# Layer 1 of a two-layer mixture of experts: gate columns of all tiles first, sixteen x buffers, fourteen tiles through the row ring

## The reference

```
x = x + 0.5 * ffn(layernorm(x))        # "layer 0"
x = x + attn(layernorm(x))             # linear recurrence over time ("mamba")
x = x + 0.5 * ffn(layernorm(x))        # "layer 1", the same weights

ffn(x):
  scores = sigmoid(gate_w @ x) + gate_b              # 16 experts
  weights, indices = top_k(scores, 4); weights /= sum
  shared = silu(x @ w1s) * (x @ w3s) @ w2s           # hidden 176
  h_e = silu((x @ w1_e) * (x @ w3_e))                # 16 experts, hidden 176
  out = shared + sum over the 4 chosen e of weight_e * (h_e @ w2_e)
```

## Time and profile before

| | |
|---|---|
| runs | 560.19, 560.35, 562.23 us, median 560.35 |
| profiled execution | 561.91 us, its span 560.1 us, mean granted TensorE clock 0.922 |
| busy share of the span | PE 86%, DVE 78%, ACT 66%, POOL 63% |
| DMA | 88.27 MB, 158 GB/s over the span |
| chain that ended last | PE 60%, DVE 16%, issue 10%, DMA 5%, POOL 4%, ACT 4% |
| layer 1 | front from 306, routing to 360.4, routed loop to 529, end to 560.1 us |

### The profile page before, as it was taken

One profiled execution on the slowest core, in us unless ns is written; L12 is line 12 of the kernel. 1 busy time (PEld: TensorE's weight loads), 2 busy tenths in 40 slices (PEclk: granted clock), 3 DMA queues, 4 the chain that ended last, 5 costly groups with the idle time before them and its releaser, 6 DMA issues.

```text
span 560.1 us, 13322 instructions
## 1 busy us (share of the span) xinstructions
PE 481.5 (86%) x3206; PEld 449.0 (80%) x3207; DVE 436.5 (78%) x1464; ACT 367.2 (66%) x1109; POOL 352.7 (63%) x364
## 2 busy tenths in 40 slices
PE   2969569999999999958996960599999999999865
PEld 2857449999999999947884950389999999999754
DVE  5889857777889888875998579656777888887836
ACT  2687836777777777767874571656777777777610
POOL 3699947546777777766411416276457777777774
PEclk9999678999999999979999885579999999999988
DMA  8992044666665566654100480036445555666666
GB/s 274 393 393 99 30 121 127 180 170 184 176 201 169 167 169 171 179 150 113 57 2 19 134 262 17 21 112 178 138 138 169 169 169 173 169 161 174 178 186 209
DMA packets 61150, 88.27 MB, mean 158 GB/s; under 512 B 9499, under 2 KB 46363, under 8 KB 61107
## 3 DMA queue, kind: packets, MB, share of 16 engines
q0 software_dynamic: 13728, 37.50, 26.3%
q1 hardware_dynamic: 47379, 50.29, 26.2%
HBM read 57.22 MB, written 30.54 MB: 157 GB/s over the span
## 4 chain that ended last, share of the span: by engine, by line
PE 60%; DVE 16%; issue 10%; DMA 5%; POOL 4%; ACT 4%; SPq 0%; POOLq 0%; ACTq 0%; DVEq 0%
PE bank L1414 29%; PE bank L1465 15%; PE bank L1435 6%; POOL mamba_room L616 3%; PE bank L1476 3%; PE bank L1475 3%; DMA ys_scratch<-ring_f 2%; DVE xres L1144 2%; PE bank L1487 1%; DMA raw_shared<-in_w13s 1%; PE bank L1633 1%; DMA ring_f<-xn_scratch,tokidx 1%; PE bank L1551 1%; DVE stage L1039 1%; DVE ring_f L1110 1%
## 5 line engine op out<-in xcount | busy, mean ns | idle before, releaser
L1465 PE MATMUL bank<-w_routed,ring_r 128*128 x790 | 120.8, 283 | 5.0 <-DVE ring_r L990 4.5
L1465 PEld LDWEIGHTS bank<-w_routed,ring_r 128*128 128x128 f32 x790 | 110.4, 189 | 7.4 <-issue 7.4
L578 POOL DMA_INDIRECT ring_f<-xn_scratch,tokidx x80 | 77.2, 965 | 58.3 <-DVE tokidx L1121 22.5
L695 ACT ACTIVATE ring_r<-bank 128x256 fp32r<-128x256 f32 x158 | 60.8, 385 | 68.9 <-PE bank L1476 66.8
L1414 PE MATMUL bank<-w_routed,ring_r 128*128 x480 | 100.6, 346 | 0.0
L578 POOL DMA_INDIRECT ring_g<-xn_scratch,tokidx x78 | 74.5, 955 | 35.4 <-PE bank L1435 20.2
L1414 PE MATMUL bank<-w_routed,ring_x 128*128 x468 | 94.6, 337 | 0.0
L1414 PEld LDWEIGHTS bank<-w_routed,ring_r 128*128 128x128 f32 x480 | 78.8, 196 | 0.1
L1414 PEld LDWEIGHTS bank<-w_routed,ring_x 128*128 128x128 f32 x468 | 74.1, 190 | 0.0
L988 DVE TENSOR_TENSOR ring_r<-bank,ring_r 128x128 fp32r<-128x128 f32 x158 | 45.8, 290 | 30.5 <-ACT ring_r L695 28.6
L547 POOL TENSOR_TENSOR w_routed<-raw_routed,w_routed 128x512 fp32r<-128x512 f32 (+1 forms) x38 | 55.3, 1494 | 19.7 <-ACT w_routed L671 19.6
(11 more groups left out here) (190 smaller groups left out, 1075.5 us busy)
## 6 DMA issues: line engine op xcount, KB each, us to landing
ys_scratch<-ring_f SPq DMA_DIRECT2D x152, 128.0 KB
raw_routed<-in_w13r SPq DMA_DIRECT2D x6, 704.0 KB, 12.2
xn_scratch<-w_routed SPq DMA_DIRECT2D x32, 128.0 KB, 4.0
raw_routed<-in_w2r SPq DMA_DIRECT2D x6, 512.0 KB, 12.7
raw_routed<-in_w13r SPq DMA_DIRECT2D x8, 352.0 KB, 6.4
xres<-in_x_in SPq DMA_DIRECT2D x4, 512.0 KB, 7.3
raw_routed<-in_w2r SPq DMA_DIRECT2D x8, 256.0 KB, 7.2
shared_scratch<-raw_ring SPq DMA_DIRECT2D x16, 128.0 KB, 1.7
```

The source lines that it names most:

```text
L578: pool.indirect_dma_start(xg[j % XG], None, xn_dram, bass.IndirectOffsetOnAxis(ap=tokidx[:, j:j + 1], axis=0)).then_inc(s_g[j % XG], 16)
L695: act.activation(hT[b][0], p_hT[b][:, 0:2 * P], ACT.Copy).then_inc(s_hhi, 1)
L1465: last = pe.matmul(p_y[b][:, 0:D], a, v, start=(q == 0), stop=(q == 4))
```

## The change

All of it concerns layer 1 (f = 1), but for one constant (`looped`) that also sets how much of ACT's loop is unrolled in layer 0.

- **Gates first.** PE does `turn_x(s)` and then `gates(s - 1)`: three-term products of the 16 gate columns alone into `p_lg`, from which ACT takes the sigmoid directly. The high and low parts of all 16 tiles are kept (`kept`) in rooms of their own.
- **Up products behind them.** `hidden` of tiles 0 to 7 (HELD = 8; 352 columns, banks 2 to 4 in turn) stands between the gates and `count`, tiles 8 to 15 behind `count`. ACT does the silu and a copy of the second half (`halves`), POOL the product (`multiply`), in place of DVE. The late experts are loaded as the kept parts they overwrite are used (one per two tiles, order 15, 14, 13, 12) and split behind tiles 7, 11 and 15. ACT switches to the sigmoid table at once instead of silu first.
- **Sixteen x buffers.** XG = (8, 16): eight more in `raw_shared` and stage 0. `lead` grows to 15 by j = 44 and falls to 4 by the end. PE's loop body has 16 steps. The shared hidden rows that lay in stage 0 are read after the loop, when all slots have been turned.
- **Fourteen tiles in the ring.** 56 rows, 44 of them in the loop, at steps 29 + 8n/7, fetched behind gather 43 + 9n/11; from n = 40 on gated by `s_y` of slot n + 24. Only tiles 14 and 15 are fetched after the last product. Shared sums 0 to 2 come behind the ring's last row, 3 to 6 behind tile 14's rows, 7 behind tile 15's.

```diff
+ADDED_FROM = 29
+EARLY_TILES = (12, 14)
+XG = (8, 16)
+IN_LOOP = (32, 44)
+BEHIND_Y, GATED = (34, 24), (28, 40)
+SUMS_AFTER = {13: (0, 1, 2), 14: (3, 4, 5, 6), 15: (7,)}
+HELD = 2 * (NE - MAMBA_E)
+LATE_AGAIN = tuple(range(NE - 1, MAMBA_E - 1, -1))
+HIGH_AFTER = {HELD - 1: LATE_AGAIN[:1], HELD + 3: LATE_AGAIN[1:2], NT - 1: LATE_AGAIN[2:]}
...
+        def early_after(f, n):
+            return 43 + 9 * n // 11 if f else max(4 * (n // TOPK) + 35, 35 + 7 * n // 5)
+        def early_step(f, n):
+            if n >= IN_LOOP[f]:
+                return NS + (n - IN_LOOP[f]) * 5 // 8
+            return ADDED_FROM + 8 * n // 7 if f else early_after(f, n)
+        def lead(f, j):
+            if f == 0 or j < 17:
+                return next(k for end, k in LEADS if j < end)
+            return min(XG[1] - 1, j * 11 // 30 + 1) if j < 44 else min(XG[1] - 1, max(4, XG[1] - (j - 43) * 2 // 5))
...  (SP)
+                for k, e in enumerate(LATE_AGAIN if f else ()):
+                    sp.wait_ge(s_h, STEPS + 2 * k + 2)
                     load_late(e)
+                    for t in range(max(0, 2 * k - 1), 2 * k + 1):
+                        hid_out(f, t)
...
-                    sp.wait_ge(s_rt, 2)
-                    for t in range(HID_AHEAD):
-                        hid_in(t)
...  (behind the loop of y_out)
+                if f:
+                    sp.wait_ge(s_xt, 2 * STEPS)
+                for t in range(HID_AHEAD if f else 0):
+                    hid_in(t)
                 for k in range(YL):
                     last_y_out(f, k)
...  (POOL)
+            def multiply(t):
+                pool.wait_ge(s_a, STEPS + t + 1)
+                pool.tensor_tensor(hidk[t], third[t], hidk[t], ALU.mult).then_inc(s_m, 1)
+                for t in range(NT if f else 0):
+                    multiply(t)
+                    for e in HIGH_AFTER.get(t, ()):
+                        low_expert(f, e)
...  (ACT)
+            def halves(t):
+                act.wait_ge(s_h, STEPS + t + 1)
+                if 4 <= t < HELD:
+                    act.wait_ge(s_m, STEPS + t - 3)
+                act.activation(hidk[t], p_hA[t % 3][:, 0:H], ACT.Silu)
+                act.activation(third[t], p_hA[t % 3][:, H:2 * H], ACT.Copy).then_inc(s_a, 1)
+                for t in range(NT if f else 0):
+                    halves(t)
+                    for e in HIGH_AFTER.get(t, ()):
+                        high_expert(f, e)
...  (PE)
+            def gates(t):
+                pe.wait_ge(s_xlo, STEPS + t + 1)
+                n = int(t >= ROUTED[1][0])
+                t0 = t - ROUTED[n][0]
+                by_token(1, t, p_lg[n][:, t0 * NE:(t0 + 1) * NE], 2 * H, NE).then_inc(s_gt, 1)
-                    if s >= 2:
+                    if f == 0 and s >= 2:
                         hidden(f, s - 2)
+                    if f == 1 and 1 <= s <= NT:
+                        gates(s - 1)
+                for t in range(HELD if f else 0):
+                    hidden(f, t)
...
                 count(f)
+                for t in range(HELD if f else NT, NT):
+                    hidden(f, t)
```

More of the change, by code:

```diff
@@ L211, in build @@
         late = [w_routed[:, g, 0, :].bitcast(f32) for g in range(MAMBA_E, NE)]
+        kept = [(2 * (LATE_AGAIN[t // 2] - MAMBA_E) + 1) * WE + t % 2 * 512 for t in range(HELD)]
+        kept = [again_late[:, k:k + 512] for k in kept]
+        kept += [ring_r[:, b * 512:(b + 1) * 512] for b in range(4)]
+        kept += [ring_x[:, b * 512:(b + 1) * 512] for b in range(2)] + [again_g[:, b * 512:(b + 1) * 512] for b in range(2)]
+        kept = [(k[:, 0:256], k[:, 256:512]) for k in kept]
+        third = [late[t % 4][:, 1024:1024 + H] for t in range(HELD)]
+        third += [room[:, b * 512 + 256:b * 512 + 256 + H] for room, n in ((raw_ring, 4), (raw_x, 2), (ring_g, 2)) for b in range(n)]
         xn = [[late[(t // 4 + 2 * f) % 4][:, t % 4 * D:(t % 4 + 1) * D] for t in range(NT)] for f in range(2)]
@@ L272, in build @@
         s_xw = [sem(f"xn_written{k}") for k in range(NG)]
-        s_g = [sem(f"gathered{k}") for k in range(XG)]
+        s_g = [sem(f"gathered{k}") for k in range(XG[1])]
         s_xt = sem("x_transposed")
@@ L349, in written, with x_before @@
             return 16 * (f * (NS - YL) // 2 + (min(n, NS - YL) - b + 1) // 2)
[L351 to L361, removed]
+        def x_before(f, k):
+            return tiles_of(k, XG[0]) if f and k < XG[0] else 0
+        def early_after(f, n):
[8 more added lines that the diff above has]
+            return min(XG[1] - 1, j * 11 // 30 + 1) if j < 44 else min(XG[1] - 1, max(4, XG[1] - (j - 43) * 2 // 5))
         def rows_fetched(f, n):
-            return f * -(-(EARLY - n % ROWS) // ROWS) + n // ROWS + 1
+            return f * -(-(EARLY[0] - n % ROWS) // ROWS) + n // ROWS + 1
         def turned(n):
@@ L819, in _ @@
                 sigmoid(f, 0)
-                for t in range(NT - 3, NT):
+                for t in range(NT - 3 if f == 0 else NT, NT):
                     logits(f, t)
@@ L826, in _ @@
                 table(SET_SILU)
-                for t in range(LAST_SILU, NT):
+                for t in range(LAST_SILU if f == 0 else NT, NT):
                     silu(f, t)
@@ L1124, in route_end @@
                     dve.wait_ge(s_et, NT)
+                else:
+                    for g in range(NG):
+                        dve.wait_ge(s_hw[g], group(0))
                 for b in range(4):
@@ L1280, in _ @@
                         scales(2, 8, NT)
-                    if t >= 4:
+                    if f == 0 and t >= 4:
                         product(f, t - 4)
@@ L1288, in _ @@
                 if f == 1:
-                    for g in range(NG):
-                        dve.wait_ge(s_hw[g], group(0))
+                    dve.wait_ge(s_hw[1], group(0))
                 else:
```

203 lines of the change are left out of this document (109 added, 94 removed).

## The result

The changed kernel took 571.86 us (median of 4 runs, 570.38 to 574.34) against 560.31 (four runs; the 560.35 of the table before was the median of three of them): ratio 1.0201, 95% interval [1.017, 1.0231]. The forecast was 557.3. The profiled execution took 570.58 us, its span 568.7 against 560.1 of before, 8.6 more.

What follows compares the result with a forecast made beforehand. It took PE to bound the routed loop, with a chained front ahead and POOL's indirect-DMA queue setting the end. Terms -6.6 + 1.7 + 1.8 = -3.1 us took the median from 560.35 to 557.3 us, range 550.5 to 563.5.

Steps and rivals of the forecast that it cites:

- Gates first: 1.7 us more: Layer 1's front: gates at 1.14 us a tile, count ending at 338.65 against 336.94, costing 1.7 us.
- the load spacing of 0.11 us: PE's gate products at low clock: weight loads bounded by 0.07 and 0.22 us, 0.11 taken, so PE not the limit.
- the fourth rival: Gates: weight loads bound them, 1.6 us a tile, count +7.9 us instead of +1.7; 563.5 us, chance 0.10.
- the first: Rival on the gates: clock up there, 0.96 us a tile, -1.8 us instead of +1.7; 553.8 us, chance 0.19.
- Low clock through the gates: PE in layer 1's gates: stays at 1.2 GHz to 327.1, granted clock 0.5.
- The eight wide tiles: PE between gates and count: 2.5 tiles at 1.84 us and 5.5 at 1.01, 10.15 us in all.
- route_slots unchanged: DVE's slot table behind the count: taken as 12.75 us.
- The second eight hidden under it: PE's wide tiles behind the count: 8.1 us run under route_slots' 12.75, costing nothing unless the clock falls.
- Picks beside POOL: 1.8 us more: Layer 1's first picks overlap POOL's low parts by 3.8 us; between 0 and 3.8, the middle taken.
- the third rival: Picks held for the whole overlap, DVE getting one operation between two of POOL's; 559.3 us, chance 0.11.
- Loop unchanged: Routed loop: PE's queue stays full and DVE's extra adds fit, so no change in time.
- End of the layer: 6.6 us less: Layer 1's end: POOL runs ahead, last fetch 540.7 against 553.3, span end 553.5 instead of 560.1.

Runs made afterwards that it cites:

- experiment 4: Changed kernel with the count behind three wide tiles instead of eight; 1.0174 of the kernel before, 572.02 us.
- tail_alone: Changed kernel with layer 1's front put back as before, new loop and end kept; 0.9887 of the kernel before, 556.76 us.
- gates_256_columns: Changed kernel with gate products of 256 columns instead of 16, the extra results unread; 1.0019 of the kernel before, 562.64 us.
- drain_adds_later: tail_alone with the drain's rows added one step later, 5 in 7 steps instead of 5 in 8; 0.9969 of the kernel before.
- twelve_tiles: tail_alone with twelve tiles and 48 rows through the ring, steps and shared-sum order as before, sixteen buffers kept; 0.9959 of the kernel before.

## Why the prediction was wrong

It failed in "Gates first: 1.7 us more", at the load spacing of 0.11 us. The bounds were 0.07 and 0.22; the value is 0.213, so the fourth rival happened, whose 1.6 us a tile, gates end at 333.3 and +7.9 us at the count stand against 1.62, 333.2 and +8.9 (the scan of DVE begins at 345.14, was at 336.97, and the front began 0.7 us earlier). The 0.11 came from transposes at the high clock and was put into a stretch that the next paragraph places at the low clock. The trace of before has the same transposes at the low clock as well: six in 1.76 us from 306.15 on, 0.27 apart, and the closest pair 0.21 apart:

```profile
309.77 0.63 PE L1487 MATMUL bank<-cst,w_routed 128*128 128x128 f32 x2
```

 The rival was weighed against with "transposes stream 128 columns as well", as if columns and not the product itself took the time; and it had a chance of only 0.10. The upper bound of 0.22 is twice the 0.11, which is what half the clock would make of it. (One of the rivals' sums is off: with 0.96 us a tile the gates of the first end at 324.9, not 325.6, which would put it at 553.1 us; it did not come true.)

- Low clock through the gates: right (0.50). The eight wide tiles, 10.15 us forecast: 10.47. route_slots unchanged, 12.87 us: right. The second eight hidden under it: right.
- "Picks beside POOL: 1.8 us more": mis-sized, 4.05 (4.36 - 0.31), the whole overlap and more than its upper end of 3.8. The overlap itself was about right (4.2, from 358.01 to 362.2). The middle averaged CASTs beside POOL's norms (0.41) and beside its low parts (1.50), but by the same paragraph only low parts lie beside the picks. The CAST reads one SBUF input, so it said nothing of two, though the prediction calls it an agreement. One DVE operation between two of POOL's, as the third rival had it, is seen in experiment 4 and not in the changed kernel, where three of POOL's passed.
- "Loop unchanged": right, 154.7 us from first to last x against 154.3.
- "End of the layer: 6.6 us less": right in its mechanism, and in tail_alone in its size (6.3). In the changed kernel's profiled execution it is 4.1: a row that took 4.2 us to land after its issue instead of 2.8 (1.4 of the 2.64 us that DVE waits) held the last product to +167.7 (forecast +166.0), and that product and the first turns ran at the low clock. The prediction had that landing as a bound.
- Sum by rows: front 8.2 (count) + 0.1 + 4.05 + 0.4 (POOL's first gather goes out 0.99 us behind the start of DVE's CAST of `tokidx`, not 0.51) = 12.7, end -4.1: 8.6, the difference of the spans.

The range reached 563.5 and left out that both front terms could stand at their upper bounds at once: 7.9 + 3.8 - 4.5 = +7.2, 567.6 us. The profiled executions differ by 8.6, the medians by 11.5.

## What to carry to other kernels

A step that shortens PE's products does not shorten PE's time below a floor per product, and it can leave PE at half clock although PE never rests: read the spacing of such products from rows at the clock of the stretch they go to, price them by the upper bound where there is no such row, and look at the granted clock after the edit. Work moved behind another engine's chain lands beside whatever that engine's neighbour does next: look for pairs of DVE and POOL that both read SBUF, and give such work to the engine that idles in a later wait. Behind a full loop, have the next stage's data there before PE asks: in three traces waits of 1 to 2 us went with several us at half clock, though in gates_256_columns a wait of 1.52 us did not. And do not price an edit from one profiled execution that is the slowest of its kernel.

## What the runs showed of the hardware

- In three-term products at 1.2 GHz the starts within a tile are 0.213 us apart with 16 columns and as much with 256, 0.307 with 368. With 256 columns a tile's six take 1.43 us, as the second start comes 0.36 us after the first, and 0.80 us at 2.4 GHz. Whether the floor is the weight load or the array was not separated.
- PE was busy for 26.26 of 27.1 us in the changed kernel's gates at a granted clock of 0.50; in gates_256_columns the clock was 0.50 to 312.9 and 0.99 from there on.
- From 529 to 542 the granted clock was 0.67, 0.74 and 0.61 in three traces with waits of 1.0 + 0.78, 1.23 and 1.56 + 0.26 us ahead of the ladder (tail_alone, drain_adds_later, twelve_tiles), and 1.00 in gates_256_columns with 1.52 + 0.15.
- One DVE operation with two SBUF inputs was held through three back-to-back operations of POOL in one kernel (4.36 us) and let in after each in another (1.09 to 1.89 us apiece, and POOL's own 512 columns took 1.45 instead of 1.25). What decides between the two stays open.
